# Attention with a spiking feed-forward layer on one core: keys, queries, key differences and the softmax shift carried in 31 instead of 76 transfers per unit

## The reference

```python
xn = layernorm(x)
q, k, v = split(xn @ w_qkv, 3)             # 16 heads of 16 features
q, k = filtered(q, mask), filtered(k, mask)  # rfft, times sigmoid(mask), irfft
attn = softmax(q @ k.T / 4)                # per batch and head, 2048 x 2048
a = (attn @ v) @ w_out + b_out
y = square(relu(xn @ W_fc.T)) @ W_proj.T   # 1024 wide
# five steps of a spiking neuron on y: mem = 0.9*mem + y - reset, spike if mem > 1
out = x + a + mean_of_spikes
```

## Time and profile before

| what | value |
|---|---|
| median of three executions | 1754.28 us |
| the profiled execution, its own time | 1755.41 us |
| its span | 1753.6 us |
| TensorE matmul busy | 1634.4 us, 93% |
| VectorE busy | 1506.6 us, 86% |
| ScalarE busy | 1177.1 us, 67% |
| GpSimd busy | 787.4 us, 45% |
| mean granted clock of TensorE | 0.977 of full speed |
| bytes moved | 156.83 MB, mean 89 GB/s |

### The profile page before, as it was taken

One profiled execution on the slowest core, in us unless ns is written; L12 is line 12 of the kernel. 1 busy time (PEld: TensorE's weight loads), 2 busy tenths in 40 slices (PEclk: granted clock), 3 DMA queues, 4 the chain that ended last, 5 costly groups with the idle time before them and its releaser, 6 DMA issues.

```text
span 1753.6 us, 60281 instructions
## 1 busy us (share of the span) xinstructions
PE 1634.4 (93%) x24366; PEld 1220.9 (70%) x24366; DVE 1506.6 (86%) x2782; ACT 1177.1 (67%) x2274; POOL 787.4 (45%) x1075
## 2 busy tenths in 40 slices
PE   9998999999999999999899999999999999999898
PEld 6566677677677677777676776776766776767677
DVE  7887898888898889889898898988988888889784
ACT  5546677677676677667676676776776676777572
POOL 2103345555444455555444455554344555544344
PEclk9999999999999999999999999999999999999999
DMA  6761233233222332333222323332223233322423
GB/s 225 231 224 47 69 87 82 66 87 83 80 67 71 84 80 71 83 85 82 68 74 75 84 65 84 85 84 73 68 76 85 70 78 86 83 69 73 134 58 100
DMA packets 150776, 156.83 MB, mean 89 GB/s; under 512 B 74464, under 2 KB 113248, under 8 KB 150496
## 3 DMA queue, kind: packets, MB, share of 16 engines
q1 hardware_dynamic: 147040, 149.75, 31.1%
q10 hardware_dynamic: 3456, 3.21, 0.6%
HBM read 119.80 MB, written 27.79 MB: 84 GB/s over the span
## 4 chain that ended last, share of the span: by engine, by line
PE 62%; DVE 16%; SPq 13%; DMA 4%; issue 3%; ACT 2%; ACTq 0%; POOL 0%; DVEq 0%; POOLq 0%
PE banks L821 22%; PE ring L773 14%; DVE pmax L1032 11%; PE ring L806 10%; PE banks L831 6%; SPq L361 4%; DMA delta_sb<-delta_scratch 4%; PE banks L826 3%; SPq L351 3%; DVE shift L1055 2%; SPq L371 2%; SPq L335 2%; ACT probs L626 2%; PE ring L942 2%; SPq L317 1%
## 5 line engine op out<-in xcount | busy, mean ns | idle before, releaser
L626 ACT ACTIVATE probs<-ring 128x512 f32<-128x512 f32 x2048 | 1076.0, 601 | 485.2 <-PE ring L806 303.7
L1032 DVE TENSOR_REDUCE pmax<-ring 128x1 f32<-128x512 f32 x2000 | 1246.5, 681 | 106.6 <-PE ring L773 98.1
L773 PE MATMUL ring<-kst,qst 64*128 64x512 f32 x2000 | 812.6, 451 | 42.3 <-DVE pmax L1032 42.3
L806 PE MATMUL ring<-qst,delta_sb 64*128 64x512 f32 x1664 | 607.9, 454 | 58.0 <-DMA delta_sb<-delta_scratch 56.4
L821 PE MATMUL banks<-probs,vst 128*32 128x128 f32 x16384 | 564.8, 279 | 0.0
L821 PEld LDWEIGHTS banks<-probs,vst 128*32 128x32 f32 x16384 | 424.1, 111 | 141.9 <-ACT probs L626 99.2
L773 PEld LDWEIGHTS ring<-kst,qst 64*128 64x128 f32 x2000 | 376.8, 188 | 180.2 <-issue 99.8
L806 PEld LDWEIGHTS ring<-qst,delta_sb 64*128 64x128 f32 x1664 | 283.1, 189 | 122.1 <-DMA delta_sb<-delta_scratch 69.8
L826 PE MATMUL banks<-xnT,wfc_sb 64*128 64x128 f32 x2016 | 279.5, 281 | 1.5 <-ACT relu_sb L631 1.5
L826 PEld LDWEIGHTS banks<-xnT,wfc_sb 64*128 64x128 f32 x2016 | 275.2, 197 | 4.9 <-ACT relu_sb L631 1.9
L831 PE MATMUL banks<-wproj_sb,hid_sb 64*128 64x256 f32 x1024 | 263.3, 377 | 0.0
(11 more groups left out here) (97 smaller groups left out, 1113.4 us busy)
## 6 DMA issues: line engine op xcount, KB each, us to landing
kst<-qk_scratch SPq DMA_DIRECT2D x256, 128.0 KB, 2.7
qst<-qk_scratch SPq DMA_DIRECT2D x256, 128.0 KB, 2.9
delta_sb<-delta_scratch SPq DMA_DIRECT2D x256, 64.0 KB, 1.9
tail<-qk_scratch SPq DMA_DIRECT2D x512, 26.0 KB, 2.2
delta_sb<-delta_scratch SPq DMA_DIRECT2D x128, 80.0 KB, 2.1
qk_scratch<-attnT SPq DMA_DIRECT2D x32, 256.0 KB, 3.0
shift_rows<-shiftT SPq DMA_DIRECT2D x512, 2.0 KB
delta_scratch<-tail SPq DMA_DIRECT2D x256, 26.0 KB, 2.0
```

The lines of the kernel that those rows point to most:

```text
L626: act.activation(probs[:, g % PS, :], score_bank(g), ACT.Exp, scale=SCALE).then_inc(exp_done, 1)
L773: pe.matmul(max_bank(x), qst[b][rows, tile * P:(tile + 1) * P], kst[b][rows, chunk * BLK:(chunk + 1) * BLK], start=True, stop=True).then_i ...
L806: pe.matmul(score_bank(g), delta_sb[rows, at:at + P], qst[b][rows, q:q + BLK], start=False, stop=True, skip_group_check=True).then_inc(sco ...
L1032: dve.tensor_reduce(pmax[:, tile, chunk:chunk + 1], max_bank(x), AX, ALU.max).then_inc(mx_taken, 1)
```

## The change

Layouts: `qk_scratch` becomes `[keys/queries, batch, head, part, feature, token]` with 384 floats of room in front, which ScalarE's queue fills once; `delta_scratch` becomes `[2, part, feature, 2048]`; a scratch in HBM for the shift is new. The differences are formed over all 2048 tokens (segments of 256 in place of 208), the first 384 of which nobody reads.

Per unit SP issues 2 transfers for the keys (8 before), 8 for the queries (8), 2 for the stage (16), 1 to store the differences (8), 4 to load them, in pieces of 128, 512, 512 and 512 tokens (12 in three pieces), 2 to store the shift and 4 to load it (16 without a scratch), and 8 for the output (8). The new `load_shift` waits on SP until the stored shift has landed. In `head`, the stage comes first, the queries move ahead of the shift, and each piece of the differences is asked for one quad earlier. On VectorE each link of `split_shift` stands behind a maximum of its own, 16 to 19 and 48 to 51, and link 1 is an addition of zeros in place of a copy.

```diff
-SEG = DELTA // SEGS
-PIECES = ((0, 5 * P), (5 * P, 9 * P), (9 * P, 13 * P))
+SEG = S // SEGS
+HEAD_ROWS = 2 * DH
+HEAD_ROOM = HOP
+PIECES = ((0, P), (P, 5 * P), (5 * P, 9 * P), (9 * P, 13 * P))
...
-        qk_dram = nc.dram_tensor("qk_scratch", [2, H, DH, 2, TOK], F32, kind="Internal").ap()
-        delta_dram = nc.dram_tensor("delta_scratch", [2, DH, 2, DELTA], F32, kind="Internal").ap()
+        qk_flat = nc.dram_tensor("qk_scratch", [HEAD_ROOM + 2 * B * H * HEAD_ROWS * S], F32, kind="Internal").ap()
+        qk_dram = qk_flat[HEAD_ROOM:].rearrange("(k b h r d t) -> k b h r d t", k=2, b=B, h=H, r=2, d=DH)
+        shift_dram = nc.dram_tensor("shift_scratch", [2, 32, P], F32, kind="Internal").ap()
+        delta_dram = nc.dram_tensor("delta_scratch", [2, 2, DH, S], F32, kind="Internal").ap()
...
-                        dst = qk_dram[w // 2, g * 8:(g + 1) * 8, :, part, t * BLK:(t + 1) * BLK].rearrange("h d t -> (h d) t")
+                        dst = qk_dram[1 - w // 2, b, g * 8:(g + 1) * 8, part, :, at:at + BLK]
...
-                keys = qk_dram[1, h, :, :, tok].rearrange("d r t -> (d r) t")
-                for group in range(4):
-                    sp.dma_start(kst[b][group * 2 * DH:(group + 1) * 2 * DH, cols].bitcast(F32),
-                                 keys).then_inc(keys_in[b][piece], 16)
+                keys = qk_dram[0, b, h:h + 1, :, :, cols].rearrange("g r d t -> g (r d) t")
+                sp.dma_start(kst[b][:, cols].bitcast(F32),
+                             keys.broadcast_to([4, HEAD_ROWS, HALF])).then_inc(keys_in[b][piece], 16)
...
-                        queries = qk_dram[0, h, :, part:part + 1, tok].broadcast_to([DH, 2, HALF])
-                        sp.dma_start(qst[b][r:r + 2 * DH, cols].bitcast(F32), queries).then_inc(queries_in[b][piece], 16)
+                        queries = qk_dram[1, b, h, part:part + 1, :, cols].broadcast_to([2, DH, HALF])
+                        sp.dma_start(qst[b][r:r + HEAD_ROWS, cols].bitcast(F32), queries).then_inc(queries_in[b][piece], 16)
...
-                for seg in range(SEGS):
-                    for k in range(2):
-                        at = b * S + k * HOP + seg * SEG
-                        sp.dma_start(stage[seg * DH:(seg + 1) * DH, k, :, :],
-                                     qk_dram[1, h, :, :, at:at + SEG]).then_inc(staged, 16)
+                for k in range(2):
+                    at = first + (k - 1) * HOP
+                    src = qk_flat[at:at + HEAD_ROWS * S].rearrange("(r c x) -> c r x", r=2, x=SEG)
+                    sp.dma_start(stage[:, k, :, :], src).then_inc(staged, 16)
...
-                for seg in range(SEGS):
-                    sp.dma_start(delta_dram[u % 2, :, :, seg * SEG:(seg + 1) * SEG],
-                                 delta_pair[seg * DH:(seg + 1) * DH]).then_inc(delta_stored, 16)
+                dst = delta_dram[u % 2].rearrange("r d (g x) -> (d g) r x", x=SEG)
+                sp.dma_start(dst, delta_pair).then_inc(delta_stored, 16)
...
-                sp.wait_ge(delta_stored, STORED * (u + 1))
-                for group in range(4):
-                    sp.dma_start(delta_sb[group * 2 * DH:(group + 1) * 2 * DH, cols].bitcast(F32),
-                                 src).then_inc(delta_in[piece], 16)
+                src = delta_dram[u % 2:u % 2 + 1, :, :, lo + HOP:hi + HOP].rearrange("g r d t -> g (r d) t")
+                sp.wait_ge(delta_stored, 16 * (u + 1))
+                sp.dma_start(delta_sb[:, lo:hi].bitcast(F32),
+                             src.broadcast_to([4, HEAD_ROWS, hi - lo])).then_inc(delta_in[piece], 16)
...
-                    for j in range(4):
-                        sp.dma_start(dst[:, :, j, :].bitcast(F32), shiftT[32 * j:32 * j + 16, :]).then_inc(shift_in, 16)
+                sp.dma_start(shift_dram[n % 2].rearrange("c (j q) -> j c q", j=4), shiftT[:, :]).then_inc(shift_stored, 16)
+
+            def load_shift(n, half):
+
+                sp.wait_ge(shift_stored, 16 * (n + 1))
+                src = shift_dram[n % 2, 0:TB, :].rearrange("(r t) x -> r (t x)", r=2)
+                for side in range(2):
+                    dst = shift_rows[side * SIDE:side * SIDE + 2, half * HALF:(half + 1) * HALF]
+                    sp.dma_start(dst.bitcast(F32), src).then_inc(shift_in, 16)
...
                 sp.wait_ge(exp_done, MINI * i + QUAD)
+                if not last:
+                    load_stage(i + 1)
                 if i and not last:
                     load_keys(h + b, 1 - b, 1)
-                if not last:
-                    load_stage(i + 1)
-                store_shift(2 * i + 1, 1)
+                    load_queries(h + b, 1 - b, 1)
+                store_shift(2 * i + 1)
+                load_shift(2 * i + 1, 1)
                 if i:
                     move_output(i - 1, 1)
-                if i and not last:
-                    load_queries(h + b, 1 - b, 1)
+                sp.wait_ge(exp_done, MINI * i + MINI // 2 + QUAD)
...
                 if not last:
                     store_delta(i + 1)
-                    store_shift(2 * i + 2, 0)
+                    store_shift(2 * i + 2)
+                    load_shift(2 * i + 2, 0)
                 if h < H - 1:
                     sp.wait_ge(exp_done, MINI * i + MINI - TB + QUAD)
                     load_keys(h + 1, b, 0)
-                move_output(i, 0)
-                if not last:
-                    for piece in range(len(PIECES)):
-                        sp.wait_ge(exp_done, MINI * i + MINI - TB + (piece + 2) * QUAD)
-                        load_delta(i + 1, piece)
+                for piece in range(0 if last else len(PIECES)):
+                    sp.wait_ge(exp_done, MINI * i + MINI - TB + (piece + 1) * QUAD)
+                    load_delta(i + 1, piece)
+                    if piece == 0:
+                        move_output(i, 0)
...
-                    dve.tensor_copy(shift[:, 0:8].bitcast(F32R), nmax[:]).then_inc(max_step, 1)
+                    if n == 0:
+                        dve.wait_ge(shift_blank, 1)
+                    dve.tensor_tensor(shift[:, 0:8].bitcast(F32R), nmax[:], shift[:, 16:24], ALU.add).then_inc(max_step, 1)
...
-                if m == LEAD - 1:
-                    for link in range(4):
-                        split_shift(link, 2 * i + 1, 1, CHUNKS * (i + 1))
+                if 0 <= m - LEAD < 4:
+                    split_shift(m - LEAD, 2 * i + 1, 1, CHUNKS * (i + 1))
...
-                if m == MINI // 2 + LEAD - 1 and not last:
-                    for link in range(4):
-                        split_shift(link, 2 * i + 2, 0, CHUNKS * (i + 1) + CHUNKS // 2)
+                if 0 <= m - LEAD - MINI // 2 < 4 and not last:
+                    split_shift(m - LEAD - MINI // 2, 2 * i + 2, 0, CHUNKS * (i + 1) + CHUNKS // 2)
```

More of the change, by code:

```diff
@@ L58 @@
 USES = 3
-KEYS = 4 * 16
+KEYS = 16
 QUERIES = 4 * 16
[L61 to L64, removed]
+SHIFT = 2 * 16
+STAGED = 2 * 16
 RUNS = 5
@@ L307, in store_block @@
                     sp.wait_ge(lo_done, QB * t + w + 1 + QK_BANKS)
+                    b, at = divmod(t * BLK, S)
                     for part in range(2):
-                        dst = qk_dram[w // 2, g * 8:(g + 1) * 8, :, part, t * BLK:(t + 1) * BLK].rearrange("h d t -> (h d) t")
+                        dst = qk_dram[1 - w // 2, b, g * 8:(g + 1) * 8, part, :, at:at + BLK]
                         sp.dma_start(dst, hilo[t % 2][w][:, part, :]).then_inc(stored[w][t % 2], 16)
             def load_keys(h, b, piece):
-                cols, tok = (slice(at + piece * HALF, at + (piece + 1) * HALF) for at in (0, b * S))
@@ L315, in load_keys @@
[L315 to L318 removed]
+                cols = slice(piece * HALF, (piece + 1) * HALF)
+                keys = qk_dram[0, b, h:h + 1, :, :, cols].rearrange("g r d t -> g (r d) t")
+                sp.dma_start(kst[b][:, cols].bitcast(F32),
+                             keys.broadcast_to([4, HEAD_ROWS, HALF])).then_inc(keys_in[b][piece], 16)
@@ L320, in load_queries @@
             def load_queries(h, b, piece):
-                cols, tok = (slice(at + piece * HALF, at + (piece + 1) * HALF) for at in (0, b * S))
+                cols = slice(piece * HALF, (piece + 1) * HALF)
                 for side in range(2):
                     for part in range(2):
-                        r = side * SIDE + part * 2 * DH
-                        queries = qk_dram[0, h, :, part:part + 1, tok].broadcast_to([DH, 2, HALF])
-                        sp.dma_start(qst[b][r:r + 2 * DH, cols].bitcast(F32), queries).then_inc(queries_in[b][piece], 16)
+                        r = side * SIDE + part * HEAD_ROWS
+                        queries = qk_dram[1, b, h, part:part + 1, :, cols].broadcast_to([2, DH, HALF])
+                        sp.dma_start(qst[b][r:r + HEAD_ROWS, cols].bitcast(F32), queries).then_inc(queries_in[b][piece], 16)
@@ L348, in load_delta @@
-                src = delta_dram[u % 2, :, :, cols].rearrange("d r t -> (d r) t")
```

(16 more changed lines are left out.)

15 lines of the change are left out of this document (11 added, 4 removed).

## The result

The changed kernel takes 1998.67 us (median of 4, 1993.66 to 2010.76) beside 1754.46 us for the kernel before on the same chip: ratio 1.140, 95% interval 1.134 to 1.146. It is slower by 14%, where 1972 us and 12% were forecast. The profiled execution has a span of 1994.8 us.

A forecast was written before the change was run, and what follows sets the result against it. TensorE was taken to wait on SP's unbroken issuing, 49.9 us a unit. After: 202 + 29 x 55.5 = 1811.5 at unit 29, 1920 at unit 31, plus 51.4: span 1971.6, forecast 1972 us, 12% slower, range 1870 to 2090.

The forecast's parts named there:

- The kernel before is bound by SP's queue: Per unit: SP issues without a break, 45 issues removed are about 29 of 49.9 us, and TensorE waits for late transfers.
- What the change removes is worth a unit of 45.2: Per unit, with SP free and no engine loaded: 45.2 us; as a rival 1596 us, 9% faster, chance 0.11.
- Outermost counts of 4, 2 and 8 mean 4, 2 and 8 engines: New transfers run on as many engines as their outermost count, always the same first ones, so narrow ones meet on two.
- 24 GB/s an engine: Rate of one DMA engine, bounds 20 to 24; rival at 21.2: 2120 us, chance 0.06; rival near 29.7: 1755 us, 0.03.
- Confirmation at 1 to 1.2 us behind a full queue: In the loop: 1 us for the first differences to land, about 1.2 for the stored shift to be written and confirmed.
- Waits of some 2 us in quad 0 and 1 to 2 in quad 1: TensorE waits there for the differences: the first piece lands at 26.1, while quad 0 wants it at 23.9.
- The wait in quad 8: TensorE waits there for `shift_rows`, some 6 us a unit, about 31 times, brought about by the new order.
- The loop of 55.5: Quad 8 to next quad 8: 14.5 of quads, shift hops, 32.2 of engine 0's work, 0.3 jitter: 55.5 us a unit.
- The sum: Whole kernel: quad 8 of unit 0 at 202, 29 units of 55.5, unit 31 at 1920, then 51.4: 1972 us.
- The order hides the load: Stated way to be wrong: landings are long but the unit is not, since the order in `head` hides them better.

The follow-up runs named there:

- e8: Kernel before the change, with only the four links of the shift each put behind a maximum of its own: 1796.34 us, ratio 1.024.
- e11: Kernel before the change, with only the four output transfers on SP moved behind the three pieces of the differences: 1776.80 us, ratio 1.011.
- e5: e1 with the output transfers moved behind all four pieces of the differences: 1620.34 us, ratio 0.923.
- e6: e5 with the scratch laid out feature before part, so prologue stores run on 16 engines, and unit loads split another way: 1597.76 us, ratio 0.910.
- e1: Changed kernel with keys, queries and differences split into transfers of 32 or 16 rows, same bytes and order: 1729.13 us, ratio 0.985.
- e7: e6 with the four links of the shift back in one lump behind maxima 15 and 47: 1675.75 us, ratio 0.956.
- e9: e7 with link 1 as a reduction of one operand in place of an addition of two: 1629.60 us, ratio 0.929.
- e10: e6 with link 1 as a reduction of one operand in place of an addition of two: 1592.43 us, ratio 0.908.
- e2: Changed kernel with only the queries split, into 8 transfers of 16 rows per half: 1851.87 us, ratio 1.055.
- e3: Changed kernel with only the keys and differences split, into 4 transfers of 32 rows each: 1805.02 us, ratio 1.028.
- e4: Changed kernel with the second half of the queries issued behind the shift's store and load, patterns unchanged: 1919.96 us, ratio 1.092.

## Why the prediction was right

The mechanism is the forecast's: narrow transfers pile up on the same few DMA engines, and the unit is as long as that pile plus TensorE's stretch from quad 8 to quad 13. That the total is so close is in part luck, since terms missed in both directions.

- **The kernel before is bound by SP's queue.** Right, and more strictly than I said (e8, e11): the two single edits at stalls only moved them.
- **What the change removes is worth a unit of 45.2.** e5 and e6 reach 45.3 and 45.1, with 57 and 52 transfers on SP in place of 31, and with the output moved last. In the order of the change itself the unit is 49.1 (e1). No run has wide transfers in the number of the change. Spreading the links is worth 78 us once SP is free (e7 to e6), 37 when link 1 is a reduction (e9 to e10), and costs 44 when SP isn't free (e8).
- **Outermost counts of 4, 2 and 8 mean 4, 2 and 8 engines.** Shown by the count of completions, to the packet, in the changed kernel and in e2, e3, e5 and e6. That they are the same engines each time, which the prediction had to assume, is shown by two busy engines under several transfers of queries, and by four under keys, differences and queries together.
- **24 GB/s an engine.** The windows give about 26.5 on two engines alone (53 / 2) and about 25 on four (97 and 106 GB/s from 686 to 690), outside the bounds of 20 to 24. What cancels it is the next term.
- **Confirmation at 1 to 1.2 us behind a full queue.** Too small. From the issue of the keys at 667.13 to TensorE's start on the first piece at 677.45 are 10.3 us. The rate of the forecast explains 5.5 + 0.7 = 6.2, start and confirmation have 4.1, where I put 1.9 (0.9 to issue and begin, 1 to land). How the 4.1 divide isn't shown.
- **Waits of some 2 us in quad 0 and 1 to 2 in quad 1.** TensorE's waits for the differences are 106.6 us, 3.4 a unit, so the sum was right. But quads 0, 1 and 2 are 3.5, 2.3 and 0.7 over their floors, 6.6 together, since the work behind the waits runs at half the clock.
- **The wait in quad 8, "6 or so".** It is 2.9 us (89.3 / 31), half of that. What was to be waited there is spent in quads 0, 1, 2 and 5 and on slow work in quads 8 and 9, ahead of or behind the wait.
- **The clock.** It has no term in the forecast. The granted clock is at half for 9.5 us of a unit (units 1 to 29). By the loop most of it should cost little, since it fills time in which TensorE would have waited for the pile (argued, no run keeps the pile and the clock apart). It should cost in the stretch from TensorE's restart in quad 8 to the issue of the next stored shift, in which no pile is waited for: 16.0 us by the mean of units 2 to 27, where the forecast has 14.5. Quads 8 and 9 are slow there (4.7 over their floors, less 2.9 of wait), and no other row accounts for the difference.
- **The loop of 55.5.** It is 56.2, and by the same mean its parts are: that stretch 16.0 (forecast 14.5), from there to the issue of the keys 2.9 (3.5), from the keys to the issue of the next shift's load 35.4 (34.3), from there to TensorE's restart 1.9 (2.9), and 0.3 for jitter that isn't needed. The pile is a little longer than forecast, with a higher rate and longer confirmations, the stretch at low clock adds 1.5, and the shift's own hops take less. Quad 5 with its 0.64 lies ahead of the wait in quad 8, while the pile still runs, and adds nothing.
- **The sum.** The largest miss is 28 x 0.7 = 20 us of pitch; 5 more lie in units 29 to 31, and 3 less in the prologue, where 202 was forecast and 199.3 measured.
- **The order hides the load.** It doesn't, in either of the two orders tried (e4).

## What to carry to other kernels

Before merging transfers, look at the outermost count of both patterns: here a copy dimension of 2 or 4 put outermost left 14 or 12 of 16 engines idle, and all such transfers queued on the same few, with a small urgent one behind them. Count the completions in the profile to see on how many engines a transfer ran. And where one queue is as long as the period, free the queue first: repairs at single stalls cost 44 us (links) and 22 us (order) while SP was full, and gained 37 to 78 and 109 us once it was free. And look at what a stall of TensorE brings with it: 2.9 us of waiting in quad 8, with the half clock behind it, put quads 8 and 9 4.7 us over their floors.

## What the runs showed of the hardware beyond what was expected

- Two lone DMA engines moved 26.5 GB/s each in rows of 4 KB (53 GB/s in all); sixteen together gave 24.8 each at best (397 in all).
- SP's issue of a narrow transfer takes longer behind a pile: four transfers of queries took SP 2.59 us at 652.20, 5.52 at 622.95 and 6.32 at 680.40, the last two straight behind keys and differences.
- A VectorE addition of 8 elements a row with two SBUF operands took 166 ns or as long as GpSimd's running instruction, up to 1.19 us; a reduction with one operand always took 161 to 163 ns in e9.
- After TensorE's wait in quad 8 the granted clock was 0.50 for the next 4 us; over the span it fell from 0.977 to 0.911, while e6, in which TensorE's matmuls wait 4.9 us for DMA in all, had 0.997 and e9 1.0.
